# Routing a graph's edges: five of a group's thirteen row one-hot columns are made by GpSimd instead of VectorE

## The reference, cut to what matters

```python
x, src, dst, edge_weight1          # (3125, 256), (103125,), (103125,), (103125, 1); dst is sorted, src is not
h = layernorm(x)
hi, hj = h[src], h[dst]
msg = silu(concatenate((hi, hj, edge_weight1)) @ mW1 + mb1)
msg = silu(layer_norm(msg, ln_g, ln_b) @ mW2 + mb2)
agg = segment_sum(msg, src, num_segments=3125)
x = x + h + silu(concatenate((h, agg)) @ uW1 + ub1) @ uW2 + ub2
# then a feed-forward layer on the top half of the nodes, chosen by a score
```

## Time and profile before

| | |
|---|---|
| time, median of 3 runs | 2336.71 us (2336.65 to 2336.82) |
| the profiled execution | 2357.2 us, of which span 2355.4 us |
| VectorE busy over the span | 1970.3 us (84%) |
| GpSimd busy over the span | 1057.2 us (45%) |
| routing, second pass: first `or_` to last indirect DMA | 162.6 to 412.2 us of the span |
| VectorE busy from 280 to 320 us | 38.97 of 40 us |
| GpSimd busy from 280 to 320 us | 9.57 of 40 us |

### The profile page before, as it was taken

The page is one execution under the profiler, slowest core; times in us unless marked ns, Lnnn a source line. Parts: engine busy times, 40 slices in busy tenths (PEclk is TensorE's granted clock), DMA queues, the critical chain, the costliest instruction groups (busy, mean ns, idle before and its releaser), DMA issues. The chain is left out here.

```text
span 2355.4 us, 52333 instructions
## 1 busy us (share of the span) xinstructions
PE 2067.4 (88%) x11942; PEld 1724.7 (73%) x11943; DVE 1970.3 (84%) x6843; ACT 1373.0 (58%) x2909; POOL 1057.2 (45%) x1088
## 2 busy tenths in 40 slices
PE   3555663499999999999999999999999999578998
PEld 2334553388888888888888888888888888455776
DVE  5899999499899999989999999998998997364970
ACT  1112330388777777777777777777777776122321
POOL 8762222555555555545545555555554551332010
PEclk9997885599999999999999999999999999788999
DMA  3000000322222222222222222222222221301000
GB/s 119 0 3 22 26 26 16 111 71 72 69 70 72 72 72 71 72 68 70 73 71 70 73 71 71 71 69 69 73 71 69 71 71 23 90 0 28 0 33 22
DMA packets 65763, 134.99 MB, mean 57 GB/s; under 512 B 20958, under 2 KB 36309, under 8 KB 65464
## 3 DMA queue, kind: packets, MB, share of 16 engines
q0 software_dynamic: 42016, 111.40, 16.6%
q1 hardware_dynamic: 22435, 22.18, 3.1%
q10 hardware_dynamic: 1266, 0.83, 0.1%
HBM read 124.20 MB, written 10.16 MB: 57 GB/s over the span
## 5 line engine op out<-in xcount | busy, mean ns | idle before, releaser
L854 POOL DMA_INDIRECT g_rows<-b_table,idx_pair x834 | 790.9, 948 | 749.7 <-DVE idx_pair L995 587.4
L965 PE MATMUL ps<-w2g,nT 128*128 128x256 f32 x3336 | 791.4, 380 | 0.0
L965 PEld LDWEIGHTS ps<-w2g,nT 128*128 128x128 f32 x3336 | 603.3, 191 | 65.2
L880 ACT ACTIVATE normed<-act,shift,rstd_e 128x255 f32<-128x255 f32 x834 | 453.7, 596 | 206.8 <-DVE shift L1067 204.3
L1004 DVE TENSOR_TENSOR agg<-psG,agg 125x256 f32 x834 | 348.9, 418 | 121.4 <-PE psG L948 53.8
L948 PE MATMUL psG<-msg,ohf 128*125 128x256 f32 x1668 | 429.0, 379 | 0.2
L901 ACT ACTIVATE nT<-psM 128x512 f32<-128x512 f32 x417 | 248.7, 596 | 117.5 <-PE psM L957 91.5
L1110 DVE BATCH_NORM_STATS2 stat_e<-act 128x6 f32<-128x256 f32 x834 | 309.9, 413 | 0.0
L1103 DVE TENSOR_TENSOR g_rows<-psH,g_rows 128x512 f32<-128x512 f32 x417 | 284.9, 683 | 23.9 <-remote 11.9
L939 PE MATMUL psH<-a_sb,ohT 128*128 x1668 | 304.2, 305 | 0.0
L948 PEld LDWEIGHTS psG<-msg,ohf 128*125 128x125 f32 x1668 | 283.4, 187 | 26.0 <-issue 0.9
(11 more groups left out here) (205 smaller groups left out, 2443.4 us busy)
## 6 DMA issues: line engine op xcount, KB each, us to landing
g_rows<-b_table,idx_pair POOLq DMA_INDIRECT x834
h_sb<-in_x SPq DMA_DIRECT2D x1, 3125.0 KB
b_table<-b_out SPq DMA_DIRECT2D x25, 125.0 KB
x_sb<-in_x SPq DMA_DIRECT2D x1, 3125.0 KB
out<-x_sb SPq DMA_DIRECT2D x5, 625.0 KB
rec_d<-rec SPq DMA_DIRECT2D x1, 1668.0 KB, 8.6
agg<-rec_d SPq DMA_DIRECT2D x6, 256.0 KB, 4.9
row<-score_d SPq DMA_DIRECT2D x1, 1525.9 KB
```

Source lines behind the costliest of these rows:

```text
L854: pool.indirect_dma_start(g_rows[:, j, n, :], None, b_table[:, :], bass.IndirectOffsetOnAxis(ap=idx_pair[:, j, n:n + 1], axis=0)).then_inc ...
L880: ins = nc.scalar.activation(normed[:, (j - 9) % 2, n, 0:D - 1], act1[:, (j - 9) % RING, n, 0:D - 1], ACT.Identity, scale=rstd_e[:, 1 - fa ...
L965: mm = pe.matmul(ps2[:, k, n, :], nT[:, k, n, q, :], w2g[:, q, :], start=(q == 0), stop=(q == 1))
```

## The change

GpSimd makes the last five of a group's thirteen one-hot columns of the row, each by one `tensor_scalar` that compares the 128 numbers of `iota_n` with a column of `r_all`. They go into a ring of four groups that lies in the memory of `f1` and `f2`, which are no longer needed then. VectorE's instruction shrinks to eight columns. TensorE waits for both. GpSimd makes the columns of groups 0 to 3 as soon as `q_all` is there, and those of group s+4 behind the indirect DMA of group s.

```diff
+PCOLS = 5
+PRING = 4
...
-            or_ = sb("or_", [P, 2, COLS, P], BF16)
+            or_ = sb("or_", [P, 2, COLS - PCOLS, P], BF16)
+            orp = [half[:, k * PCOLS * P // 2:(k + 1) * PCOLS * P // 2].bitcast(BF16).rearrange("p (t r) -> p t r", t=PCOLS)
+                   for half in (f1, f2) for k in range(PRING // 2)]
...
+                def pool_columns(s):
+                    if s >= PRING:
+                        pool.wait_ge(s_win, s - PRING + 1)
+                    for k in range(PCOLS):
+                        c = s * COLS + COLS - PCOLS + k
+                        ins = pool.tensor_scalar(orp[s % PRING][:, k, :], iota_n[:, :], r_all[:, c:c + 1], None,
+                                                 ALU.is_equal)
+                    ins.then_inc(s_orp, 1)
+
+                pool.wait_ge(s_places, 1)
+                for s in range(PRING):
+                    pool_columns(s)
                 pool.wait_ge(s_upto, 1)
                 pool.tensor_tensor(upto[:, :, :], upto[:, :, :], tot[:, :, :], ALU.subtract).then_inc(s_jump, 1)
...
                                             recw[:, s % 4, :, :].rearrange("p w n -> p (w n)"), None).then_inc(s_scat, 16)
+                    if s + PRING < SUPERS:
+                        pool_columns(s + PRING)
...
                     pe.wait_ge(s_or, s + 1)
+                    pe.wait_ge(s_orp, s + 1)
...
-                        mm = pe.matmul(psK[:, s % 3, 0:PLANES * WIN], or_[:, s % 2, t, :],
+                        marks = or_[:, s % 2, t, :] if t < COLS - PCOLS else orp[s % PRING][:, t - COLS + PCOLS, :]
+                        mm = pe.matmul(psK[:, s % 3, 0:PLANES * WIN], marks,
...
-                link(V.tensor_tensor(q_all[:, :], place[:, :], f2[:, :], ALU.subtract))
+                V.tensor_tensor(q_all[:, :], place[:, :], f2[:, :], ALU.subtract).then_inc(s_places, 1)
+                dve.wait_ge(s_places, 1)
...
-                    V.tensor_tensor(or_[:, s % 2, :, :], r_all[:, own].unsqueeze(2).broadcast_to([P, COLS, P]),
-                                    iota_v.unsqueeze(1).broadcast_to([P, COLS, P]), ALU.is_equal)
+                    mine = slice(s * COLS, (s + 1) * COLS - PCOLS)
+                    V.tensor_tensor(or_[:, s % 2, :, :],
+                                    r_all[:, mine].unsqueeze(2).broadcast_to([P, COLS - PCOLS, P]),
+                                    iota_v.unsqueeze(1).broadcast_to([P, COLS - PCOLS, P]), ALU.is_equal)
```

More of the change, by code:

```diff
@@ L220, in build @@
             s_or = sem("s_or")
+            s_orp = sem("s_orp")
+            s_places = sem("s_places")
             s_win = sem("s_win")
```

## The result

The changed kernel takes 2380.16 us (median of 4 runs, 2373.91 to 2380.77), the kernel before 2336.77 us; the ratio is 1.018 with a 95% interval of 1.0162 to 1.0197. It is 43 us slower. Forecast were 12 us slower, with a range that reached to 45. The way was right and GpSimd's loop did become the pace; the size was not right, because a turn of that loop was priced too low and a wait at group 52 was taken to be hidden. The trace of the changed kernel is of its shortest execution, 2373.91 us; the other three took 2380.03 to 2380.77 us.

A forecast was written before the change was run, and what follows sets the result against it. VectorE was taken to pace the routing stage's second pass at 3.78 us a group; GpSimd's 3.84 us turns would then pace, putting the last indirect DMA at 424.4 us, 12 us later: 2349 us, range 2306 to 2382.

The forecast's parts named there:

- What bounds the kernel now, and what VectorE gives up: Routing stage, second pass: VectorE paces at 3.78 us a group; `or_` shrinks 0.645 us, giving up 40 us at most.
- What GpSimd takes on: GpSimd's loop: five comparisons 2.65 us, indirect DMA 0.957, gap 0.23; 3.84 us a turn, above VectorE's 3.13.
- the rival's 0.76: Gap ahead of GpSimd's indirect DMA: 0.76 us each time if the DMA's preparation doesn't overlap with the comparisons.
- The start: Ahead of the loop: 20 comparisons (10.4 us) delay the chain for `dest`; first indirect DMA at 194.2, bounds 191 and 198.
- ScalarE's wait at group 52 stays hidden: Routing loop, group 52: ScalarE's 11.36 us wait is covered by GpSimd's four groups of lead, 15.4 us.
- The sum: Last indirect DMA: 194.2 + 58 x 3.84 + 3 x 2.48 = 424.4 us against 412.24, 12 us later; 2349 us.
- The signs: Expected in the changed trace: `or_` near 1.23 us, comparisons near 0.57, DMAs 3.84 apart, VectorE idle 0.7 a group before `or_`.
- The cheap comparison: GpSimd's loop: comparison at 289 ns, turn 2.43 us, VectorE stays the pace, faster; 2307 us, chance 0.33.
- The break-even: GpSimd's loop: comparison of 0.51 to 0.545 us leaves the end within 5 us; 2337 us, chance 0.10.
- The dear case: GpSimd's loop: comparison dearer by 0.1 us or more, or bare 0.76 us DMA preparation; 2380 us, chance 0.13.

The follow-up runs named there:

- the kernel with the trials: Changed kernel plus 24 GpSimd instructions behind its last indirect DMA, four each of six kinds; also the second trace of the routing code; 2388.57 us, one execution.

## Why the prediction was right about the way and wrong about the size

**What bounds the kernel now, and what VectorE gives up.** Right. `or_` fell by 663 ns, 645 were reckoned. The kernel in which VectorE gives up nothing takes the same time.

**What GpSimd takes on.** Right that its loop becomes the pace; the turn was mis-sized, 4.21 us for 3.84, and this is the main step that failed:

- Five comparisons take 2.94 us instead of 2.65. In the steady loop, 205 to 445 us, their row is

```profile
L481 POOL TENSOR_SCALAR f<-iota_n,r_all 128x128 bf16<-128x128 bf16 x279 | 164.0, 601 | 2.6
```

  One lasts 0.601 us where the line of the earlier trace rows gave 0.57; that is 5 x 0.031 = 0.16 us. The overlap of neighbours, 0.05 in the forecast, I had carried over from the earlier trace rows, from a memset and from a pair of different kinds. Among comparisons it is (5 x 0.601 - 2.94) / 4 = 0.016 us; that is 4 x 0.034 = 0.14 us. The two are about equal parts of the 0.29 us.
- The indirect DMA takes 1.05 instead of 0.957 us behind comparisons, also the one of 444.04, which has none behind it; 0.05 us pass from its end to the next comparison. No indirect DMA of the routing stage stood behind a comparison before.
- The gap ahead of it is 0.17 us (0.23 forecast, between 0.16 and 0.30), so the first of the two bounds held and the rival's 0.76 did not.

Together 0.37 us a turn, times 58, are 21.5 us.

**The start.** Right in the trace, and partly by luck: first indirect DMA at 194.13, forecast 194.2. The chain ended at 186.64 and VectorE waited 0.38 us for it. The comparisons began at 158.55, three microseconds earlier than I had allowed, and took 14.77 us instead of 10.4, since the first, beside VectorE's scan, took 3.7 us. `w2g` was blocked as feared (3.57 us for two), and `tb_i` wasn't (0.24 us). How long `w2g` is held differs from trace to trace, and with it the start: in the second trace of the same routing code it took 5.22 us and the first indirect DMA started at 196.53.

The run with `w2g` moved, 3.76 against 0.76 us, agrees with the rule of the Trainium skill on the shared port pair (SBUF — State Buffer, Who interferes with whom), and so does `oqv`: with one input in SBUF, it stayed at 1457 ns beside a GpSimd busy 95% of the time. What the runs show is the waiting; that the ports are the reason is the skill's.

**ScalarE's wait at group 52 stays hidden.** This step failed, by 5.55 us. I looked at the wait in the earlier trace rows as ScalarE's and compared it with GpSimd's lead over `recw`, which did cover it. But the transfer for which ScalarE waits also holds up the landing of the indirect DMA issued behind it, and GpSimd waits for each landing before its next issue. Four groups of lead over `recw` are no lead over a landing. In the kernel before, this lay under GpSimd's idle time. Moving the transfer removed the wait; that run removes ScalarE's wait as well, so it is the row of the changed kernel (releaser: the landing) that tells the two apart: `recw` of the group after 404.83 had been ready since 397.82. With three columns it is ScalarE's wait itself that shows (9.18 us, releaser `recw`).

**The sum.** 424.4 + 21.5 + 5.55 = 451.5, the measured start of the last indirect DMA. It is 39.2 us later than before; the medians differ by 43.4. The trace is of the shortest of the changed kernel's four executions, 6 us below the others. The second trace of the same routing code has that DMA 1.8 us later, at 453.28, all of it and a little more from its later start; where the rest of the 4 us lies stays open.

**The signs.** VectorE was to wait 0.7 us a group ahead of `or_`. It waits 19.0 us in 62 groups there, 0.3 us a group, and 53.4 us ahead of `low`, where it waits for ScalarE's copy.

**The rivals.** The cheap comparison did not come about: a copy costs 294 ns, a comparison twice that. Nor does the rule of the Trainium skill (GPSIMD Engine Reference, Engine selection) hold here for TENSOR_SCALAR, which takes 2.5 ns an element on GpSimd against VectorE's 1.0; for the copy it is near (294 ns for 128 elements, and 1519 ns for the 1280 of L1313 in the node stage, of another type, which is 1.06 ns an element). The break-even needed a turn of 3.63 us. The kernel with four columns has one of 3.62 us, and its last indirect DMA started 6.2 us late (418.42), which the wait at group 52, 6.09 us there, accounts for. The dear case's time came true, 2380, by luck: its reasons were a comparison dearer by 0.1 us or more and a bare gap of 0.76 us, and 0.03 and 0.17 us were measured.

## What to carry to other kernels

When work moves to an engine that now waits most of the time, price every small thing in the turn of its loop by rows in which the same kinds of instruction stand next to each other: an overlap of 0.05 us that was taken from other kinds, on four seams, made 0.14 us a turn here, and the loop has 58 turns. Then look for every wait that the idle time has been hiding there, also for the landings of its DMAs. The number of items moved is a dial, and the balance is where both loops are equal: here three columns, not five, made the kernel 0.4% faster, and 0.9% with the two waits out of the way that the move had uncovered.

## What the runs showed of the hardware that I had not expected

- TENSOR_SCALAR of 128 elements on GpSimd starts every 0.59 us, whether a row lasts 528 ns (constant) or 604 (scalar from SBUF), in the kernel with the trials.
- An indirect DMA of this stage lasts 1.05 us when the instruction ahead of it on GpSimd is a comparison, also with nothing behind it (444.04), and 0.96 us when it is another indirect DMA, also with comparisons right behind it (453.28 in the kernel with the trials).
- An indirect DMA issued 2.3 us behind a transfer of 3.5 KB on another queue, which itself took 10.7 us to land, landed so late that its successor started 9.8 us after it, in place of 4.2.
- ScalarE, busy 12 of 40 us, could not take 1.5 us a group while the tables are made: two groups went from 7.6 to 10.2 us. From group 50 on the same columns cost nothing (3.18 us a group, whether ScalarE or GpSimd makes them).
